# Attention kernel on one Trainium2 core: the first group's maxima computed inside the last half batch of projections

## The chip, the cores and the metric

One core of one Trainium2 chip runs the kernel. The metric is the device time of one execution in microseconds (us), the median of three runs: 2611.24 us for the kernel before (2609.54 to 2612.29).

## The reference, cut to what matters

One transformer layer with adaptive layer norm; x is 4 x 1024 x 1024 in float32.

```
mod = silu(c) @ wmod                        # six parts: sa, ca, ga, sb, cb, gb
h   = layernorm(x) * (1 + ca) + sa
q, k, v = h @ Wq, h @ Wk, h @ Wv            # 32 query heads, 8 key/value heads, head size 32
q, k = rope(q), rope(k)
att = q @ k.T / sqrt(32), causal            # 4 query heads share one key/value head
x   = x + ga * ((softmax(att) @ v) @ Wo)
h   = layernorm(x) * (1 + cb) + sb
x   = x + gb * (h @ W.T + bias + lora)
```

## The kernel before, in words

Three functions run one after the other, each with a program block of its own, and at a block's end all engines meet: `qkv` (projections), `attention`, `linear_half`.

**qkv** works on eight half batches m of 512 tokens. For each, PE multiplies twelve chunks of 128 output columns (two of k, two of v, eight of q, `project`, L502 to L514): 24 matmuls a chunk, since weights and activations are each split into a high and a low part. For the ten chunks of k and q, ACT copies the product out of PSUM (L317), DVE applies the rotary embedding (`rotate`, L402 to L411: a product, a shuffle, a product, a sum), ACT rounds to the high part (L329), POOL subtracts for the low part (L469), and SP stores both to DRAM in `qk_t` (L242). v is transposed and stored to `v_t` (L249). During half batch m the activations of m + 1 are normalized and transposed; the last half batch has nothing of that kind beside it. At the end SP waits until all stores have landed (L279 to L281).

**attention** works on 32 groups n (4 batches x 8 key/value heads, 4 query heads each). A group needs, from DRAM, stacked copies of q and k (high, high and low parts, 96 rows; `load_stack`, L643). Softmax needs each row's maximum before the exponential, so a group's scores are computed twice: first with queries on the partitions, in 38 units (`max_scores`, L968 to L984), each reduced by DVE (`take_max`, L844); the maxima are then split into high and low (L853), transposed by PE (`turn`, L1002), copied by ACT (L811) and written by SP as two more rows of the q stack (L655); then, with keys on the partitions, in 20 units (`scores`, L948) which subtract the maximum through these two rows, ACT's exponential (L792), the product with v (`values`, L986) and sums. L977 and L983 add the causal mask by a product with the identity.

The order on every engine is one list, `STEPS` (L130): first all 38 units of group 0, its turn and the 10 first units of group 1, alone; from there on each group's scores are mixed with the maxima of the next ones. `SP` first loads stacks 0 and 1, v of batch 0 and one 4 MB part of wmod (L720 to L723), then follows the list. The three PSUM banks for maxima, turns and sums are used in turn.

Of the kernel before, what the change touches and what calls it, by code (L numbers as in the profile page):

```python
# [14 lines left out]
P = 128  # L15
# [23 lines left out]
XB = 4  # L39
# [90 lines left out]
STEPS = [("max", 0, m) for m in range(NM)] + [("turn", 0)] + [("max", 1, m) for m in range(NM) if MAX_TICK[m] < 0]  # L130
STEPS += [s for n in range(NG + 1) for s in group_steps(n)]
# [29 lines left out]
def qkv(nc, consts, x_in, wq_in, wk_in, wv_in, c_in, wmod_in, silu_cols, mod_cols, rope_in, qk_out, v_out):  # L161
# [3 lines left out]
    with ExitStack() as ctx:  # L165
# [3 lines left out]
        w = [sb("w_hi", [P, NC, DC, P], F32R), sb("w_lo", [P, NC, DC, P], F32R)]  # L169
        with ExitStack() as first:  # L170
            def early(name, shape):
                return first.enter_context(nc.sbuf_tensor(name, shape, F32))

            wm = early("wm", [P, DC, 4, HALF])
            crow, erow, srow = (early(n, [B, D]) for n in ("c_rows", "c_exp", "c_silu"))
            mrows = early("mod_rows", [P, HALF])
        h = [[sb(f"h_hi{i}", [P, DC, HALF], F32R), sb(f"h_lo{i}", [P, DC, HALF], F32R)] for i in range(2)]
        qst = [sb(f"roped_hilo{i}", [P, 2, HALF], F32R) for i in range(QST)]
        vst = sb("v_rows", [P, 4, P])
        qf = [sb(f"proj_raw{i}", [P, HALF]) for i in range(QF)]  # L180
        qc, rot = sb("proj_cos", [P, HALF]), sb("proj_rot", [P, HALF])
        xt = [sb(f"x_in{i}", [P, D]) for i in range(XB)]
        rope = sb("rope", [P, 2, T])
        hf = [sb(f"h_raw{i}", [P, HALF]) for i in range(TPS)]
        stats, mv, sd = sb("stats", [P, 4, 12]), sb("mean_var", [P, 4, 2]), sb("std", [P, 4, 4])
        ident = consts[:, 0:P]
        raw = [sb(f"w_raw{i}", [P, DC, P]) for i in range(STAGES)]
# [5 lines left out]
        ups = ctx.enter_context(nc.psum_tensor("mod_turned", [P, HALF], F32))  # L193

# [15 lines left out]
        s_qs = [count(f"qk_stored{i}", 16) for i in range(QST)]  # L210
        s_vs = count("v_stored", 16)
# [10 lines left out]
        def _(sp):  # L222
# [6 lines left out]
            def load_w(c):  # L229
                i = c % STAGES  # L230
                if c >= STAGES:
                    sp.wait_ge(s_wl.sem, s_wl.at(c - STAGES + 1))
                kind, n = CHUNKS[c]
                src = {"q": wq_in, "k": wk_in, "v": wv_in}[kind]
                sp.dma_start(raw[i][:, :, :],
                             src[:, n * P:(n + 1) * P].rearrange("(k p) n -> p k n", p=P)).then_inc(s_raw[i].sem, 16)
# [15 lines left out]
            def load_wm(k):  # L252
                sp.dma_start(wm[:, k, :, :], wmod_in[k * P:(k + 1) * P, 0:4 * HALF].rearrange("p (q n) -> p q n", q=4)
                             ).then_inc(s_wm[k].sem, 16)
# [24 lines left out]
            for i in range(QST):  # L279
                sp.wait_ge(s_qs[i].sem, s_qs[i].at(len([r for r in range(NRP * HB) if r % QST == i])))  # L280
            sp.wait_ge(s_vs.sem, s_vs.at(2 * HB))  # L281

        @block.scalar
        def _(act):
# [10 lines left out]
            def w_hi(c):  # L295
                i = c % STAGES
                act.wait_ge(s_raw[i].sem, s_raw[i].at(c // STAGES + 1))
                nc.scalar.activation(w[0][:, c, :, :], raw[i][:, :, :], ACT.Copy
# [46 lines left out]
            for m in range(HB):  # L345
                for c in range(NC):
# [7 lines left out]
                    if m + 1 < HB:  # L354
# [5 lines left out]
                        for k in TURN_H.get(c, ()):  # L360
                            h_hi(m + 1, k)
                rope_hi(m, NC - 1)

        @block.vector
        def _(dve):
# [72 lines left out]
            for m in range(HB):  # L438
                for c in range(NC):
                    if m + 1 < HB:  # L440
                        for k in TURN_H.get(c, ()):
                            modulate(m + 1, k)
                    if CHUNKS[c][0] != "v":
# [9 lines left out]
        def _(pool):  # L453
            def w_lo(c):
                i = c % STAGES
                pool.wait_ge(s_wh.sem, s_wh.at(c + 1))
                nc.gpsimd.tensor_tensor(w[1][:, c, :, :], raw[i][:, :, :],
                                        w[0][:, c, :, :].bitcast(F32), ALU.subtract).then_inc(s_wl.sem, 1)
# [19 lines left out]
            for m in range(HB):  # L478
                for c in range(NC):
# [10 lines left out]
        def _(pe):  # L490
# [11 lines left out]
            def project(m, c):  # L502
# [5 lines left out]
                for k in range(DC):  # L508
                    if c == 0:
                        pe.wait_ge(s_hl.sem, s_hl.at(DC * m + k + 1))  # L510
                    for n, (a, i) in enumerate(((0, 0), (0, 1), (1, 0))):
                        last = nc.tensor.matmul(pps[e % PPS][:, :], w[a][:, c, k, :], h[m % 2][i][:, k, :],  # L512
                                                start=(k == 0 and n == 0), stop=(k == DC - 1 and n == 2))
                last.then_inc(s_pj.sem, 1)  # L514

# [14 lines left out]
            for k in range(DC):  # L530
                pe.wait_ge(s_wm[k].sem, s_wm[k].at(1))
                for q in range(4):
                    last = nc.tensor.matmul(mps[DH * q:DH * (q + 1), :], silu_cols[:, k, :], wm[:, k, q, :],
# [21 lines left out]
def attention(nc, consts, qk_in, v_in, wmod_in, silu_cols, mod_cols, modv, pre, cs, wo_in, la_in, lb_in, lw_in, s_pre, ctx_out, sums_out, inv_t):  # L555


    with ExitStack() as ctx:
# [3 lines left out]
        qs = sb("q_stack", [P, QS, G, T], F32R)  # L562
        ks = sb("k_stack", [P, QS, T], F32R)
        V = sb("v", [P, 2, TT, KV * DH])
# [4 lines left out]
        negm = sb("neg_max", [P, 2, G, TT])  # L569
        mfull = sb("neg_max_and_hi", [P, G * TT, 2])  # L570
        mhl = sb("neg_max_hilo", [P, P], F32R)
        mrow = sb("neg_max_rows", [2 * G * TT, P], F32R)
        maskS = sb("mask_q_k", [P, G, P], F32R)
        maskT = sb("mask_k_q", [P, G, P], F32R)
        identr = sb("ident_r", [P, P], F32R)
# [11 lines left out]
        def count(name, step=1):  # L587
# [3 lines left out]
        s_st = [count(f"stack_loaded{i}", 16 * 6) for i in range(QS)]  # L591
        s_v = [count(f"v_loaded{i}", 16) for i in range(2)]
        s_p1, s_mx, s_mc, s_mh, s_ml, s_mt, s_me = (count(n) for n in (
            "max_scores", "max_taken", "max_joined", "max_hi", "max_lo", "max_turned", "max_rows"))
        s_mr = [count(f"max_stacked{i}", 32) for i in range(QS)]
# [41 lines left out]
        def _(sp):  # L637
            def load_v(b):
                if b >= 2:
                    sp.wait_ge(s_pv.sem, s_pv.at(NQ * KV * (b - 1)))  # L640
                sp.dma_start(V[:, b % 2, :, :], v_in[b].rearrange("(i p) d -> p i d", p=P)).then_inc(s_v[b % 2].sem, 16)

            def load_stack(n):  # L643
                b, g, s = n // KV, n % KV, n % QS
                if n >= QS:
                    sp.wait_ge(s_p2.sem, s_p2.at(NE * (n - QS + 1)))
                for row, part in enumerate((0, 0, 1)):
                    sp.dma_start(qs[DH * row:DH * row + DH, s, :, :].bitcast(F32),
                                 qk_in[b, HEADS_Q + g, part].rearrange("(h d) t -> d h t", d=DH)).then_inc(s_st[s].sem, 16)
                for row, part in enumerate((0, 1, 0)):  # L650
                    k = DH * (g % HEADS_K)
                    sp.dma_start(ks[DH * row:DH * row + DH, s, :].bitcast(F32),
                                 qk_in[b, g // HEADS_K, part, k:k + DH, :]).then_inc(s_st[s].sem, 16)

            def stack_max(n):  # L655
                sp.wait_ge(s_me.sem, s_me.at(n + 1))
                for i in range(2):
                    sp.dma_start(qs[MHI + i:MHI + i + 1, n % QS, :, :].rearrange(
                        "a h (i n) -> a (h i) n", n=P).bitcast(F32),
                                 mrow[G * TT * i:G * TT * (i + 1), :].bitcast(F32)).then_inc(s_mr[n % QS].sem, 16)  # L660
# [841 lines left out]
```

## Time and profile before

| what | value |
|---|---|
| median of three runs | 2611.24 us |
| the profiled execution | 2611.64 us |
| its span, first to last instruction | 2609.9 us |
| PE busy | 2514.4 us (96%) |
| DVE busy | 1577.4 us (60%) |
| POOL busy | 1649.7 us (63%) |
| ACT busy | 1021.0 us (39%) |
| PE's last projection matmul ends | 614.8 us |
| first matmul of the maxima of group 0 | 635.5 us |
| first scores matmul of group 0 | 668.8 us |

PE is TensorE's matmuls and PEld its weight loads, DVE is VectorE, ACT ScalarE, POOL GpSimd, SP the engine that issues the DMAs. The granted clock of PE is given as a share of 2.4 GHz: 1.00 is 2.4 GHz and 0.50 is 1.2 GHz.

### The profile page before, as it was taken

The page shows a single profiled execution, that of the slowest core. Times are in us where ns is not written, and L with a number is a line of the kernel's source. Part 1 is how long each engine was busy: PE and PEld are TensorE (multiplying, and loading weights), DVE is VectorE, ACT ScalarE, POOL GpSimd, SP SyncE. Part 2 cuts the span into 40 slices and gives each one's busy share as a digit, 9 for nine tenths or more (in the row PEclk, how much of TensorE's full clock was granted, in tenths as well). Part 3 has the DMA queues.
Part 4 walks back from the last instruction along what each step waited for, and adds up shares of the span by engine and source line. Part 5 has one row for each costly group of instructions (what it writes and reads, how often), then busy time and mean ns, then how long its engine had stood idle before and what let it go on. Part 6 is the DMA issues. An engine that isn't in the chain of part 4 may idle for free. (4 is left out here: it accounts for less than half of the span.)

```text
span 2609.9 us, 37478 instructions
## 1 busy us (share of the span) xinstructions
PE 2514.4 (96%) x14476; PEld 1871.7 (72%) x14476; DVE 1577.4 (60%) x2509; ACT 1021.0 (39%) x1301; POOL 1649.7 (63%) x863
## 2 busy tenths in 40 slices
PE   5999999996999999999999999899899999999998
PEld 2788888885766666666666666565588788888886
DVE  4667666655766666666666666465755455454553
ACT  3333333321455665565555666465411111111110
POOL 4543333331488898988988889787555455555553
PEclk8999999997799999999999999899999999999999
DMA  7432233325324335225332335230433433333330
GB/s 277 137 114 103 99 114 113 113 89 173 95 74 131 79 81 139 76 67 144 83 91 53 71 81 161 56 79 19 161 97 97 111 91 97 108 95 105 113 89 25
DMA packets 179726, 267.53 MB, mean 103 GB/s; under 512 B 20508, under 2 KB 113884, under 8 KB 178400
## 3 DMA queue, kind: packets, MB, share of 16 engines
q1 hardware_dynamic: 179552, 265.13, 34.5%
q8 instruction: 119, 1.95, 0.3%
q14 instruction: 55, 0.45, 0.1%
HBM read 183.22 MB, written 80.81 MB: 101 GB/s over the span
## 5 line engine op out<-in xcount | busy, mean ns | idle before, releaser
L927 POOL TENSOR_TENSOR p_sum<-p_sum,p_ring 128x1024 f32<-128x1024 f32 (+2 forms) x465 | 993.9, 2171 | 188.5 <-PE ctx_ps L997 170.4
L850 DVE TENSOR_REDUCE neg_max<-scores_q 128x1 f32<-128x512 f32 (+3 forms) x1216 | 740.6, 658 | 390.8 <-PE scores_q L983 226.5
L792 ACT ACTIVATE p_ring<-scores 128x1024 f32<-128x1024 f32 (+2 forms) x512 | 463.6, 918 | 250.4 <-PE scores L965 178.9
L979 PE MATMUL scores_q<-k_stack,q_stack 96*128 96x512 f32 (+3 forms) x1536 | 467.5, 381 | 0.4 <-DVE prefetched L892 0.4
L961 PE MATMUL scores<-q_stack,k_stack 98*128 98x512 f32 (+1 forms) x1216 | 417.4, 421 | 12.7 <-ACT p_ring L792 11.8
L469 POOL TENSOR_TENSOR roped_hilo<-roped_hilo 128x512 fp32r<-128x512 f32 x80 | 104.3, 1304 | 333.2 <-ACT roped_hilo L329 333.2
L961 PEld LDWEIGHTS scores<-q_stack,k_stack 98*128 98x128 f32 x1216 | 195.5, 192 | 166.1 <-issue 96.2
L979 PEld LDWEIGHTS scores_q<-k_stack,q_stack 96*128 96x128 f32 x1536 | 284.7, 198 | 38.1 <-DVE neg_max L850 4.2
L512 PE MATMUL proj_ps<-h_hi,w_hi 128*128 128x512 f32 x768 | 304.6, 397 | 1.6 <-POOL h_lo L462 1.6
L512 PE MATMUL proj_ps<-h_hi,w_lo 128*128 128x512 f32 x768 | 300.2, 391 | 0.0
L512 PE MATMUL proj_ps<-h_lo,w_hi 128*128 128x512 f32 x768 | 300.0, 391 | 0.0
L1354 POOL TENSOR_TENSOR h_scaled<-h_scaled,mod_now 128x512 f32<-128x512 f32 x64 | 65.6, 1046 | 328.1 <-DVE h_scaled L1299 328.0
L997 PE MATMUL ctx_ps<-p_ring,v 128*32 128x512 f32 (+3 forms) x2560 | 233.0, 473 | 0.0
L1426 PE MATMUL pf<-we_hi,h_hi 128*128 128x512 f32 x512 | 201.3, 393 | 8.6 <-POOL h_lo L1358 8.6
L1426 PE MATMUL pf<-we_hi,h_lo 128*128 128x512 f32 x512 | 200.8, 392 | 0.0
L1426 PE MATMUL pf<-we_lo,h_hi 128*128 128x512 f32 x512 | 200.7, 392 | 0.0
L1379 PE MATMUL po<-wo_hi,ctx_hi 128*128 128x512 f32 x496 | 196.8, 397 | 0.0
L792 ACT ACTIVATE p_sum<-scores 128x1024 f32<-128x1024 f32 x128 | 131.1, 1025 | 164.0 <-PE scores L965 93.7
L1379 PE MATMUL po<-wo_hi,ctx_lo 128*128 128x512 f32 x496 | 194.0, 391 | 0.0
L1379 PE MATMUL po<-wo_lo,ctx_hi 128*128 128x512 f32 x496 | 193.7, 391 | 0.0
L317 ACT COPY proj_raw<-proj_ps 128x512 f32<-128x512 f32 x96 | 56.4, 587 | 333.2 <-PE proj_ps L512 333.2
L983 PE MATMUL scores_q<-mask_q_k,ident_r 128*128 128x128 f32 x768 | 175.5, 229 | 0.0
(147 smaller groups left out, 3722.3 us busy)
## 6 DMA issues: line engine op xcount, KB each, us to landing
q_stack<-qk_t SPq DMA_DIRECT2D x96, 512.0 KB, 6.9
qk_t<-roped_hilo SPq DMA_DIRECT2D x80, 512.0 KB, 2.7
x_in<-in_L_attn_resid SPq DMA_DIRECT2D x32, 512.0 KB, 6.3
prefetched<-in_L_wmod SPq DMA_DIRECT2D x4, 4096.0 KB, 13.9
ctx_t<-ctx_raw SPq DMA_DIRECT2D x64, 256.0 KB, 4.5
prefetched<-ctx_t SPq DMA_DIRECT2D x31, 512.0 KB, 4.1
prefetched<-inv_t SPq DMA_DIRECT2D x124, 128.0 KB, 5.4
k_stack<-qk_t SPq DMA_DIRECT2D x96, 128.0 KB, 8.8
```

The lines of the kernel that those rows point to most:

```text
L469: nc.gpsimd.tensor_tensor(lo, lo.bitcast(F32), qst[r % QST][:, 0, :].bitcast(F32), ALU.subtract).then_inc(s_rl.sem, 1)
L512: last = nc.tensor.matmul(pps[e % PPS][:, :], w[a][:, c, k, :], h[m % 2][i][:, k, :], start=(k == 0 and n == 0), stop=(k == DC - 1 and n = ...
L792: nc.scalar.activation(probs(n, u), src, ACT.Exp, scale=SM_SCALE).then_inc(s_ex.sem, 1)
L850: nc.vector.tensor_reduce(negm[:, lo // HALF, hs[0]:hs[-1] + 1, i:i + 1], src, AX.X, ALU.max, negate=True).then_inc(s_mx.sem, 1)
L927: nc.gpsimd.tensor_tensor(a, a, probs(n, u), ALU.add).then_inc(s_ap.sem, 1)
L961: last = nc.tensor.matmul(o[a], ks[0:KS, n % QS, j * P:(j + 1) * P], qs[0:KS, n % QS, h0:h0 + per, lo:lo + w], start=True, stop=not diag)
L979: last = nc.tensor.matmul(dst[:, a, :], qs[0:MHI, n % QS, h, i * P:(i + 1) * P], ks[0:MHI, n % QS, lo:lo + w], start=not first, stop=not d ...
L983: last = nc.tensor.matmul(dst[:, a, w - P:w], identr[:, :], maskS[:, 0, :], start=False, stop=True)
L997: last = nc.tensor.matmul(cps[DH * h:DH * (h + 1), lo - hf * HALF:HALF], V[:, b % 2, j, g * DH:(g + 1) * DH], p[:, a, :], start=(j == 0), ...
L1354: nc.gpsimd.tensor_tensor(v, v, cur[:, 4 * h:4 * h + 4, 1:2].broadcast_to([P, 4, P]), ALU.add).then_inc(s_hf.sem, 1)
L1379: last = nc.tensor.matmul(po[h][:, :], cs[slot][a][:, k, :], wo[w][:, k, h * HALF:(h + 1) * HALF], start=(k == 0 and n == 0), stop=(k == D ...
L1426: mm = nc.tensor.matmul(pf[h][:, :], hs[a][:, k, :], we[w][:, k, h * HALF:(h + 1) * HALF], start=(k == 0 and n == 0), stop=(k == DC - 1 an ...
```

## The change

The 38 maxima units of group 0, its turn, and the 10 first units of group 1 leave `STEPS` and are made in `qkv` during the last half batch (m = 7): 48 units, placed behind the matmuls of chosen k steps of chunks 1 to 11 (four a chunk, six in chunks 3 and 4). Four PSUM banks that the last half batch doesn't need hold them. DVE reduces a chunk's units ahead of that chunk's `rotate`. The turn is made at chunk 10, ACT's copy behind it, and SP writes the two rows at chunk 11.

For this the memory is laid out anew: `Early` holds tiles of `qkv` that are dead by the end of half batch 6, and `Shared` lies in the same place with stacks 0 and 1, v, the masks and the tiles of the maxima. SP fetches stack 0 in half batch 6 at chunk 9, and stack 1 and v at the start of half batch 7. The wait for all stores at the end of `qkv` goes; waits for stores are put ahead of the loads that need them, and ahead of the first exponential that writes the ring of probabilities. `attention` begins with 4 mask copies on ACT in place of 9, a memset of one k tile in place of three, and its list begins with the scores of group 0. The 4 MB part of wmod is now loaded at the start of group 1.

The diff, cut to its core:

```diff
-STEPS = [("max", 0, m) for m in range(NM)] + [("turn", 0)] + [("max", 1, m) for m in range(NM) if MAX_TICK[m] < 0]
-STEPS += [s for n in range(NG + 1) for s in group_steps(n)]
+STEPS = [s for n in range(NG + 1) for s in group_steps(n)]
+FIRST_MAXIMA = [(0, m) for m in range(NM)] + [(1, m) for m in range(NM) if MAX_TICK[m] < 0]
+UNIT_AT = {}
+for _c in range(1, NC):
+    for _k in (range(1, DC - 1) if _c in (3, 4) else range(1, DC, 2)):
+        if len(UNIT_AT) < len(FIRST_MAXIMA):
+            UNIT_AT[len(UNIT_AT)] = (_c, _k)
+TURN_FIRST = NM + 2
...
+def max_product(nc, sh, qs, ks, bank, m):
+    i, lo, w, hs, diag = MAX_UNITS[m]
+    dst = bank[:, 0:len(hs) * w].rearrange("p (h n) -> p h n", h=len(hs))
+    first = diag and w == P
+    if first:
+        nc.tensor.matmul(dst[:, :, :], sh.identr, sh.maskS[:, 0:len(hs), :], start=True, stop=False)
+    for a, h in enumerate(hs):
+        last = nc.tensor.matmul(dst[:, a, :], qs[0:MHI, h, i * P:(i + 1) * P], ks[0:MHI, lo:lo + w],
+                                start=not first, stop=not diag or first and a == len(hs) - 1)
+        if diag and not first:
+            last = nc.tensor.matmul(dst[:, a, w - P:w], sh.identr, sh.maskS[:, 0, :], start=False, stop=True)
+    last.then_inc(sh.s_p1.sem, 1)
...
 # qkv, SP
+                    if (m, c) == (HB - 2, 9):
+                        sp.wait_ge(s_tp.sem, s_tp.at(DC * HB))
+                        sp.wait_ge(s_wl.sem, s_wl.at(NC))
+                        for i in range(QST):
+                            sp.wait_ge(s_qs[i].sem, s_qs[i].at(len([r for r in range(2 * NRP) if r % QST == i])))
+                        fetch_stack(sp, sh, sh.qs[0], sh.ks[0], qk_out, 0)
+                    if (m, c) == (HB - 1, 0):
+                        sp.wait_ge(s_pj.sem, s_pj.at(NC * (HB - 1)))
+                        fetch_stack(sp, sh, sh.qs[1], sh.ks[1], qk_out, 1)
+                        sp.wait_ge(s_vs.sem, s_vs.at(4))
+                        fetch_v(sp, sh, v_out, 0)
+                    if (m, c) == (HB - 1, UNIT_AT[TURN_FIRST][0] + 1):
+                        stack_rows(sp, sh, sh.qs[0], 0)
...
-            for i in range(QST):
-                sp.wait_ge(s_qs[i].sem, s_qs[i].at(len([r for r in range(NRP * HB) if r % QST == i])))
-            sp.wait_ge(s_vs.sem, s_vs.at(2 * HB))
...
 # qkv, ACT
+                if m == HB - 1:
+                    act.wait_ge(s_hl.sem, s_hl.at(DC * HB))
+                    nc.scalar.activation(sh.identr, ident, ACT.Copy).then_inc(sh.init.sem, 1)
+                    for i in range(G):
+                        nc.scalar.activation(sh.maskS[:, i, :], consts[:, P:2 * P], ACT.Copy).then_inc(sh.init.sem, 1)
...
+                    if m == HB - 1 and c == UNIT_AT[TURN_FIRST][0]:
+                        act.wait_ge(sh.s_mt.sem, sh.s_mt.at(1))
+                        nc.scalar.activation(sh.mrow, vps[0:2 * G * TT, 0:P], ACT.Copy).then_inc(sh.s_me.sem, 1)
...
 # qkv, DVE
+                    if m == HB - 1:
+                        for i, (n, unit) in enumerate(FIRST_MAXIMA):
+                            if UNIT_AT[i][0] == c:
+                                max_reduce(nc, dve, sh, max_banks[i % len(max_banks)], n, unit)
+                                if i == NM - 1:
+                                    max_split(nc, dve, sh, 0)
                     if CHUNKS[c][0] != "v":
                         rotate(m, c)
...
 # qkv, PE: called behind the three matmuls of step (c, k) of project(7, c)
+            def first_max(i):
+                if i == 0:
+                    pe.wait_ge(sh.init.sem, sh.init.at(G + 5))
+                n, m = FIRST_MAXIMA[i]
+                if m == 0:
+                    pe.wait_ge(sh.s_st[n].sem, sh.s_st[n].at(1))
+                if i >= len(max_banks):
+                    pe.wait_ge(sh.s_mx.sem, sh.s_mx.at(i - len(max_banks) + 1))
+                max_product(nc, sh, sh.qs[n], sh.ks[n], max_banks[i % len(max_banks)], m)
+                if i == TURN_FIRST:
+                    pe.wait_ge(sh.s_ml.sem, sh.s_ml.at(1))
+                    pe.wait_ge(s_vc.sem, s_vc.at(2 * HB))
+                    nc.tensor.transpose(vps[:, 0:P], sh.mhl.bitcast(F32), ident).then_inc(sh.s_mt.sem, 1)
...
 # attention, SP
-            load_stack(0)
-            load_stack(1)
-            load_v(0)
-            load_part(0)
             for step in STEPS:
                 kind, n = step[0], step[1]
                 if kind == "scores" and step[2] == 0:
                     if n + 2 < NG:
                         load_stack(n + 2)
+                    if n == 1:
+                        load_part(0)
...
 # attention, ACT
-            nc.scalar.activation(identr[:, :], consts[:, 0:P], ACT.Copy).then_inc(init.sem, 1)
             for h in range(G):
-                nc.scalar.activation(maskS[:, h, :], consts[:, P:2 * P], ACT.Copy).then_inc(init.sem, 1)
                 nc.scalar.activation(maskT[:, h, :], consts[:, 2 * P:3 * P], ACT.Copy).then_inc(init.sem, 1)
...
+                    if n == 0 and place == 0 and not before:
+                        for i in range(QST):
+                            act.wait_ge(sh.s_qs[i].sem, sh.s_qs[i].at(len([r for r in range(NRP * HB) if r % QST == i])))
+                        act.wait_ge(sh.s_vs.sem, sh.s_vs.at(2 * HB))
...
 # attention, POOL and PE
-            nc.gpsimd.memset(ks[MHI:MHI + DH, :, :].bitcast(F32), 1.0).then_inc(init.sem, 1)
+            nc.gpsimd.memset(ks[2][MHI:MHI + DH, :].bitcast(F32), 1.0).then_inc(init.sem, 1)
...
-            pe.wait_ge(init.sem, 2 * G + 5)
+            pe.wait_ge(init.sem, G + 2)
```

## Rows read from the trace of the kernel before

**Rows 1.** Windows by stage: PE, PEld, DVE, ACT, POOL busy, granted clock, DMA share.
```profile
549.40:614.80 65.40, 65.36 (x293) 53.77 (x291) 29.80 (x50) 12.58 (x24) 12.89 (x10) 1.00 0.24 89
614.80:635.50 20.70, 0.00 (x0) 0.00 (x0) 3.32 (x8) 3.65 (x12) 5.18 (x3) 0.57 0.63 165
635.50:661.60 26.10, 24.62 (x75) 18.73 (x75) 23.39 (x42) 0.00 (x0) 0.00 (x0) 0.50 0.83 262
661.60:668.80 7.20, 7.20 (x29) 6.80 (x29) 5.12 (x9) 1.55 (x2) 0.00 (x0) 0.50 0.50 121
668.80:682.50 13.70, 13.70 (x47) 11.48 (x49) 8.01 (x13) 5.29 (x6) 0.00 (x0) 0.50 0.39 83
704.50:740.00 35.50, 35.49 (x257) 23.61 (x256) 23.69 (x43) 21.20 (x25) 31.99 (x16) 1.00 0.30 73
```

**Rows 2.** Timeline between the last projection and the first maxima: start, duration, what.
```profile
619.37 1.26 POOL L469 TENSOR_TENSOR roped_hilo<-roped_hilo 128x512 fp32r<-128x512 f32 x1 [2.11 <-ACT roped_hilo L329]
...
623.86 1.30 SPq L648 DMA_DIRECT2D q_stack<-qk_t  x3
623.86 2.65 POOL L916 MEMSET k_stack<- 32x3072 f32 x1 [3.23 <-POOLq L165]
623.88 0.31 ACT L768 ACTIVATE ident_r<-consts 128x128 fp32r<-128x128 f32 x1 [4.59 <-PEq L165]
...
625.20 1.48 SPq L652 DMA_DIRECT2D k_stack<-qk_t  x3
...
625.49 0.29 ACT L771 ACTIVATE mask_k_q<-consts 128x128 fp32r<-128x128 f32 x1
...
635.55 0.77 PE L977 MATMUL scores_q<-mask_q_k,ident_r 128*128 128x512 f32 x1 [20.79 <-DMA k_stack<-qk_t]
```

**Rows 3.** SP's wait for the landing of the stores, line L281.
```profile
L281 SPq EVENT_SEMAPHORE  x1: 2271/2271/2271, 621.1 to 621.1; - x1
```

**Rows 4.** Groups by form in 636 to 661.5 us: the most frequent of DVE's reduces.
```profile
L850 DVE TENSOR_REDUCE neg_max<-scores_q 128x1 f32<-128x512 f32 x24 | 14.8, 684 | 0.1
```

**Rows 5.** Timeline: first scores and first values of group 0.
```profile
668.80 1.16 PE L961 MATMUL scores<-q_stack,k_stack 98*128 98x512 f32 x2
...
681.94 1.31 PE L997 MATMUL ctx_ps<-p_sum,v 128*32 128x512 f32 x8
```

**Rows 6.** Timeline of PE at full clock: starts of masked maxima matmuls of 128, 256 and 512 columns.
```profile
805.07 0.45 PE L977 MATMUL scores_q<-mask_q_k,ident_r 128*128 128x512 f32 x1
...
805.98 0.33 PE L979 MATMUL scores_q<-k_stack,q_stack 96*128 96x256 f32 x1
...
808.79 0.33 PE L979 MATMUL scores_q<-k_stack,q_stack 96*128 96x256 f32 x1
...
809.02 0.33 PE L979 MATMUL scores_q<-k_stack,q_stack 96*128 96x256 f32 x1
...
1143.03 0.45 PE L979 MATMUL scores_q<-k_stack,q_stack 96*128 96x512 f32 x1
1143.31 0.22 PE L983 MATMUL scores_q<-mask_q_k,ident_r 128*128 128x128 f32 x1
1143.37 0.45 PE L979 MATMUL scores_q<-k_stack,q_stack 96*128 96x512 f32 x1
```

**Rows 7.** Waits of the queues, 600 to 640 us: who waited, total, times, longest.
```profile
SPq L242 <- POOL roped_hilo L469: 23.2, 5, 5.1
```

**Rows 8.** The page's DMA issues: count, KB each, median us to landing.
```profile
k_stack<-qk_t SPq DMA_DIRECT2D x96, 128.0 KB, 8.8
```

**Rows 9.** Windows of 1 us, columns of rows 1: where the granted clock falls and rises.
```profile
617.00:618.00 1.00, 0.00 (x0) 0.00 (x0) 0.87 (x2) 0.00 (x0) 0.26 (x1) 0.82 0.00 0
...
90.00:91.00 1.00, 0.68 (x3) 0.68 (x4) 0.00 (x0) 1.00 (x3) 0.44 (x1) 0.50 0.00 0
...
95.00:96.00 1.00, 1.00 (x5) 0.79 (x4) 1.00 (x3) 0.00 (x0) 1.00 (x1) 0.80 0.00 0
...
682.00:683.00 1.00, 1.00 (x9) 0.27 (x12) 0.69 (x1) 0.00 (x0) 0.00 (x0) 0.75 0.00 0
```

More of the change, by code:

```diff
@@ L158, in at, with __init__, sb @@
         return k * self.step
-def qkv(nc, consts, x_in, wq_in, wk_in, wv_in, c_in, wmod_in, silu_cols, mod_cols, rope_in, qk_out, v_out):
+class Early:
+    def __init__(self, nc, ctx):
+        def sb(name, shape, dt=F32):
+            return ctx.enter_context(nc.sbuf_tensor(name, shape, dt))
+        self.w_hi = sb("w_hi", [P, NC, DC, P], F32R)
+        self.xt = [sb(f"x_in{i}", [P, D]) for i in range(XB)]
+        with ExitStack() as before:
+            self.wm0 = before.enter_context(nc.sbuf_tensor("wm0", [P, DC // 2, 4, HALF], F32))
+        self.h0 = [sb("h_hi0", [P, DC, HALF], F32R), sb("h_lo0", [P, DC, HALF], F32R)]
+        self.raw = [sb(f"w_raw{i}", [P, DC, P]) for i in range(STAGES)]
+        self.hf = [sb(f"h_raw{i}", [P, HALF]) for i in range(TPS)]
@@ new lines, in fetch_stack @@
+def fetch_stack(sp, sh, qs, ks, qk_in, n):
+    b, g, s = n // KV, n % KV, n % QS
+    for row, part in enumerate((0, 0, 1)):
+        sp.dma_start(qs[DH * row:DH * row + DH, :, :].bitcast(F32),
+                     qk_in[b, HEADS_Q + g, part].rearrange("(h d) t -> d h t", d=DH)).then_inc(sh.s_st[s].sem, 16)
+    for row, part in enumerate((0, 1, 0)):
+        k = DH * (g % HEADS_K)
+        sp.dma_start(ks[DH * row:DH * row + DH, :].bitcast(F32),
+                     qk_in[b, g // HEADS_K, part, k:k + DH, :]).then_inc(sh.s_st[s].sem, 16)
@@ L779, in exp @@
                 else:
-                    _, before = ring_place(n, u)
+                    place, before = ring_place(n, u)
+                    if n == 0 and place == 0 and not before:
+                        for i in range(QST):
+                            act.wait_ge(sh.s_qs[i].sem, sh.s_qs[i].at(len([r for r in range(NRP * HB) if r % QST == i])))
+                        act.wait_ge(sh.s_vs.sem, sh.s_vs.at(2 * HB))
                     if before:
@@ L1449, in _ @@
                 sp.wait_ge(s_k, 16)
-        qkv(nc, consts, x, wq, wk, wv, c, wmod, silu_cols, mod_cols, rope, qk_t, v_t)
+        with ExitStack() as first:
+            early = Early(nc, first)
         pre = ctx.enter_context(nc.sbuf_tensor("prefetched", [P, DC + 2, D], F32))
@@ L1453, in build @@
         s_pre = [ctx.enter_context(nc.semaphore(n)) for n in ("wo_fetched", "first_ctx_fetched", "first_ctx_ready",  "lora_fetched", "lora_a_scaled")]
-        attention(nc, consts, qk_t, v_t, wmod, silu_cols, mod_cols, modv, pre, cs, wo, la, lb, lw, s_pre, ctx_t, sums_t, inv_t)
+        with ExitStack() as both:
+            sh = Shared(nc, both)
+            qkv(nc, early, sh, consts, x, wq, wk, wv, c, wmod, silu_cols, mod_cols, rope, qk_t, v_t)
+            attention(nc, sh, consts, qk_t, v_t, wmod, silu_cols, mod_cols, modv, pre, cs, wo, la, lb, lw, s_pre, ctx_t, sums_t, inv_t)
         linear_half(nc, consts, x, pre, cs, s_pre, w, bias, modv, mod_cols, ctx_t, sums_t, inv_t, out)
```

206 lines of the change are left out of this document (109 added, 97 removed).

## The prediction

> **What bounds the kernel now.** I read the table of windows by stage first. In the last half batch of projections PE is busy 65.36 of 65.40 us at a clock of 1.00, and in a steady stretch of attention 35.49 of 35.50 us [rows 1]: in both, PE is the bound. Between them it isn't. PE stands still for 20.7 us, then makes the maxima of group 0 in 26.1 us and the ten first units of group 1 in 7.2 us, all at 0.50, which is 1.2 GHz. From the last projection (614.8) to the first scores (668.8) pass 54.0 us.
>
> The timeline says what these consist of. The last chunk's way through ACT, DVE, ACT and POOL ends at 620.6 [rows 2]; SP then issues the last store and waits 2.27 us for its landing [rows 3]; the new block begins at 623.86; its copies and memsets end by 626.5, but PE is held until 635.55, and the row names the DMA of a k stack [rows 2]. Loads, not setup, end that wait. In the maxima themselves DVE is the pace: busy 23.39 of 26.1 us [rows 1], with 24 reduces of 512 columns at 684 ns and hardly any idle time [rows 4], while PE waits for banks. In 661.6 to 668.8 PE is the bound, at half clock.
>
> DVE, meanwhile, has room just before: 29.80 us busy in the 65.4 us of the last half batch [rows 1]. So the change takes work that is bound by DVE and by a DMA, alone, and puts it where PE is the bound. There it costs PE's time for it, and nothing else if DVE and SP keep up.
>
> **The change part by part.** The sum is made for the profiled execution (2611.64 us, 0.4 us above the median).
>
> 1. *Removed:* everything from 614.8 to 668.8, 54.0 us [rows 1, 2, 5].
>
> 2. *PE's time for 48 units and a transpose inside the half batch.* Prices are from start to start at full clock [rows 6]. Two masked matmul pairs of 256 columns begin 0.23 us apart (808.79, 809.02), of 512 columns 0.34 us (1143.03, 1143.37); I take 0.29 for 384 columns, between the two. A unit of four heads with 128 columns is 0.68 us: from 805.07 to 805.98 lie it and one pair of 256, so 0.91 - 0.23. A 512 without a mask costs up to the 0.28 us from 1143.03 to the mask's start at 1143.31; the 512 columns alone are 0.213 us at 2.4 GHz; I take 0.24. Group 0 has 2 units of the 128 kind, 8 pairs each of 256, 384 and 512, and 16 plain 512: 1.36 + 1.84 + 2.32 + 2.72 + 3.84 = 12.1 us. The ten of group 1 are 0.68 + 4 x 0.23 + 4 x 0.29 + 3 x 0.34 = 3.8 us. With the transpose, 16.0 us. No row shows these units between projection matmuls, so I bound it: below by the columns alone (22,528 + 6,528 over 2.4 GHz = 12.1 us), above by the 33.3 us that they take now at half clock behind DVE [rows 1]. I stay at 16.0, since rows 6 too have other matmuls before and behind.
>
> 3. *DVE beside it, costed at nothing.* DVE gets 48 reduces at 0.68 us at most, 33 us, to its 29.8: 63 us in a stage of 65.4 + 16.0 = 81.4. Per chunk of four units: PE 5.45 + 1.33 = 6.8 us, DVE 4 x 0.68 + 3.0 = 5.7. A unit waits only for the reduce four units back, which for four a chunk is the same place in the chunk before, and that reduce stands ahead of that chunk's rotate: done. Behind the reduces wait rotate, then ACT's and POOL's rounding and the store; they have three PSUM banks and three stage tiles of slack. Chunks 3 and 4, with six units, follow the v chunks, which have no rotate. If this cover were gone, each us of DVE over 6.8 a chunk would be a us of PE.
>
> 4. *SP and the loads.* Stack 0 is six DMAs, issued at chunk 9 of half batch 6: 2.8 us of SP's time by the like six from 623.86 on (1.30 + 1.48 [rows 2]), against an idle of up to 5.1 us between stores [rows 7]. Landing takes about 9 us [rows 8], and PE wants it at chunk 1 of half batch 7, about four chunks (22 us) later. Stack 1 and v (seven DMAs, some 3.3 us) go in the same way and are wanted at chunk 9. The stores of q and k behind them start at most 3 us late; rotate needs a store only three chunks later. Two rows of maxima are written at chunk 11, which ends before the block does. Cost zero; if late, PE would stand still for the lateness, not more. ACT's five mask copies (1.2 us) delay one PSUM copy by half a us, with three banks behind it. POOL's two memsets (0.9 us each, a third of the 2.65 us [rows 2]) fall into half batch 1, where POOL has most of its time free.
>
> 5. *The new boundary.* Before: PE's end to the new block 623.86 - 614.8 = 9.1 us. The landing wait of 2.3 us [rows 3] goes; the wait that replaces it stands on ACT before its third exponential, over 4 us into the block, when the store has long landed. The last unit's reduce stands ahead of the last rotate: +0.5. So 7.3 us. Then four copies on ACT: nine took 1.9 us (623.88 to 625.78 [rows 2]), 0.2 apart after a first of 0.31, so 0.9; POOL's memset takes 0.9 beside them; with 0.2 for the semaphore and the first weights, the first scores stand 1.1 us into the block. PE's gap is 8.4 us.
>
> 6. *Attention from its first scores on* is the same list. The clock will have fallen: it fell 2.8 us after PE's last matmul [rows 9]. Before, it was at 0.50 from the first scores for 13.7 us more, until 682.5 [rows 1, 9]. I take the same: its rise came 0.6 us after the first values matmuls (681.94 [rows 5]), and these stand at the same place of the list in both kernels, while the 21 us of maxima and scores before them, with PE never idle, brought no rise. The bound on the other side is under the rivals. The first table load of ACT (1.3 us) overlaps the first scores.
>
> 7. *The 4 MB part of wmod* moves from the start to group 1. It no longer shares the DMA engines with the first stacks; it will share them with stack 3, which is wanted some 26 us later, and the part itself is wanted at group 4, over 100 us later. Nothing.
>
> Sum: 54.0 - 16.0 - 7.3 - 1.1 = 29.6 us saved. 2611.6 - 29.6 = 2582.0 for an execution like the profiled one, **2581.6** against the median of 2611.24.
>
> **The rivals.**
>
> *The clock rises sooner (0.25).* After another stop, the projections begin again at 90.3 and the clock is up at about 95.4, 5.1 us later [rows 9]. Should it do so in the new ramp, 13.7 - 5.1 = 8.6 us of half-clock work shrink to no less than half: 4.3 us more, 2577.3. Against it: the same kind of work ran at 0.50 for 21 us. The Trainium skill ("TensorE: Matmul & The Clock Gate", on the clock gate) says that how busy PE has been recently sets the clock, which alone would bring it up soon after any restart; the trace agrees at 90 us and not at 661 us.
>
> *The units cost PE more between projections (0.12).* Each unit switches the array from 128 to 96 rows and to a mask, or DVE's semaphores come late now and then. At 24 to 26 us for the 48 units, about midway between 16.0 and the 33.3 of now, the gain is 20 to 22 us: 2590.
>
> *DVE becomes the bound of the last half batch, and the kernel is slower (0.03).* Place: DVE's queue, where the reduces of a chunk stand ahead of its rotate. It decides from 6.8 us of DVE a chunk on; to be slower than before, the half batch must take 111 us, 10.1 a chunk of the eleven. That needs rotate and reduces to take 1.8 times 5.7 us, as by a held-up chain over stores. At 11 us a chunk: 2611 + 10 = 2621. For it: all ten rotates wait on a chain of four engines. Against it: DVE's shuffles and reduces keep their times in every stage that I read.
>
> *The gap stays (0.02).* If the first scores had to wait again for something issued only in the new block, the 9 to 20 us of waiting would come back, and with a dearer item 2 almost all would be eaten: about 2608.
>
> **How the numbers follow.** My case has 0.58, the early clock 0.25, dearer units 0.12, slower 0.03, the gap 0.02. A measurement of this kernel can tell about 0.2%, 5.2 us, from no change. Faster by over that: 0.58 + 0.25 + 0.12 and half of the last, 0.96; within it 0.01; slower 0.03. The range takes in the early clock with a cheaper item 2 (2577.3 less 1 to 2) and reaches on the other side to item 2 at 22 us: 2575.5 to 2588. Dearer units, the gap and the slower case beyond it, and an early clock with the columns' bound, make up less than 0.2.
>
> **What would show it.** In the changed profile: the last half batch lasts 81 to 82 us with PE busy throughout at 1.00 and no idle time put down to neg_max; DVE busy some 63 us in it; no row with a wait for k_stack; PE's gap about 8.4 us; the clock at 0.50 from the gap until the first values. Wrong would be: PE waits for neg_max between projections (rival three); a first scores matmul later than 640.5; a rise of the clock 5 us after it (rival one); a stage of over 86 us with PE busy (rival two).

## The result and the profile after

The changed kernel takes 2578.49 us (median of four runs, 2577.02 to 2580.00) against 2611.76: a ratio of 0.9873, interval 0.9856 to 0.9890. Run again beside other kernels, it took 2581.36 against 2611.10: 0.9886, 0.9870 to 0.9901. So the saving is 30 to 33 us; 29.6 was forecast, at 2581.6.

Windows by stage of the changed kernel, with the columns of [rows 1]:

```profile
549.40:632.00 82.60, 82.58 (x395) 68.63 (x393) 59.00 (x103) 13.97 (x30) 14.11 (x10) 1.00 0.37 107
632.00:639.60 7.60, 0.00 (x0) 0.00 (x0) 3.71 (x7) 2.41 (x8) 3.73 (x3) 0.66 0.30 113
639.60:651.60 12.00, 11.99 (x37) 10.35 (x38) 5.94 (x9) 5.92 (x6) 0.00 (x0) 0.50 0.84 180
651.60:670.00 18.40, 18.40 (x131) 11.80 (x133) 12.90 (x25) 11.92 (x13) 14.85 (x8) 1.00 0.04 16
```

The last half batch was 65.4 us and is 82.6, with PE busy throughout at 1.00 and DVE at 59.0 us. Of the three lines between it and the first scores in [rows 1] one is left, 7.6 us.

The timeline across the boundary, to be read beside [rows 2, 5]:

```profile
631.71 0.58 ACT L442 COPY proj_raw<-proj_ps 128x512 f32<-128x512 f32 x1 [5.56 <-PE proj_ps L661]
631.75 0.22 PE L247 MATMUL turn_ps<-mask_q_k,ident_r 128*128 128x128 f32 x1
632.01 0.69 DVE L257 TENSOR_REDUCE neg_max<-turn_ps 128x1 f32<-128x512 f32 x1 [1.06 <-PE turn_ps L247]
...
636.54 1.26 POOL L612 TENSOR_TENSOR roped_hilo<-roped_hilo 128x512 fp32r<-128x512 f32 x1 [2.12 <-ACT roped_hilo L454]
...
638.61 0.95 POOL L1038 MEMSET k_stack<- 32x1024 f32 x1 [0.80 <-POOLq L280]
...
639.61 1.22 PE L1083 MATMUL scores<-q_stack,k_stack 98*128 98x512 f32 x2 [7.63 <-POOL k_stack L1038]
...
652.27 1.07 PE L1107 MATMUL ctx_ps<-p_sum,v 128*32 128x512 f32 x8
```

The first scores stand at 639.6 in place of 668.8, and the row names POOL's memset, not a DMA, as what PE waited for last. The saving to this point is 29.2 us. The span is 33.9 us shorter, so another 4.7 us came later. The account by stages stands in the table below.

Every kernel profiled, by stage (us). "Front" runs from the first projection matmul to the first scores matmul; "attention" from there to the first DMA of `linear_half`; "linear" from that to the issue of the last store but one of the output; "clock" is how long after the first scores the granted clock reached 1.00 (0: it never fell); "jump" is the longest record of the branch that closes PE's loop in `linear_half`. That branch runs three times: it jumps back twice and falls through once.

| kernel | front | attention | linear | clock | jump |
|---|---|---|---|---|---|
| before | 620.0 | 1171.6 | 745.8 | 13.7 | 7.2 |
| changed | 590.8 | 1169.9 | 743.2 | 12.0 | 6.5 |
| e1_fetch_only | 607.1 | 1170.7 | 743.8 | 12.8 | 6.7 |
| e2_end_wait | 594.0 | 1170.0 | 745.8 | 12.0 | 6.9 |
| e3_two_reduces | 606.1 | 1172.3 | 745.4 | 14.3 | 6.9 |
| e4_warm | 590.3 | 1169.0 | 739.9 | 11.0 | 0.2 |
| e5_warm31 | 591.7 | 1165.3 | 738.4 | 0 | 0.2 |
| e6_tiny26 | 590.7 | 1170.2 | 739.7 | 12.1 | 0.2 |
| e7_group1_left | 593.6 | 1169.4 | 743.1 | 11.4 | 6.2 |
| e8_part_early | 591.5 | 1168.9 | 746.4 | 11.0 | 7.3 |
| e9_tail_units | 590.8 | 1162.9 | 739.6 | 0 | 0.2 |
| e10_before_tiny26 | 621.0 | 1170.3 | 737.3 | 12.3 | 0.2 |
| e11_after_again | 591.1 | 1170.4 | 746.2 | 12.5 | 6.8 |
| e12_warm31_again | 591.7 | 1165.6 | 738.3 | 0 | 0.2 |

What is left of each span is the time up to the first projection matmul, which varied from 48.5 to 51.0 us between kernels that do the same there, and 22 to 24 us behind the issue of the last store but one.

### The profile page after: what moved, and what is told of

The parts are those of the page before. It is cut to its first block and busy times, and to the rows that moved or that the text cites. A ratio compares the mean times of both kernels' runs of the same rounds, so it can differ in the third digit from the quotient of the medians.

```text
span 2576.0 us, 37491 instructions
## 1 busy us (share of the span) xinstructions
PE 2494.8 (97%) x14476; PEld 1858.3 (72%) x14476; DVE 1581.7 (61%) x2509; ACT 1020.0 (40%) x1301; POOL 1649.5 (64%) x865
## 5 line engine op out<-in xcount | busy, mean ns | idle before, releaser
L257 DVE TENSOR_REDUCE neg_max<-scores_q 128x1 f32<-128x512 f32 (+1 forms) x1168 | 711.5, 658 | 375.6 <-PE scores_q L247 227.6
L244 PE MATMUL scores_q<-k_stack,q_stack 96*128 96x512 f32 (+1 forms) x1473 | 436.6, 371 | 0.1
L244 PEld LDWEIGHTS scores_q<-k_stack,q_stack 96*128 96x128 f32 x1473 | 265.7, 192 | 32.2 <-DVE prefetched L1014 0.9
L661 PEld LDWEIGHTS proj_ps<-h_hi,w_lo 128*128 128x128 f32 x768 | 144.7, 188 | 31.2
```

The lines of the kernel that those rows point to most:

```text
L244: last = nc.tensor.matmul(dst[:, a, :], qs[0:MHI, h, i * P:(i + 1) * P], ks[0:MHI, lo:lo + w], start=not first, stop=not diag or first and ...
L257: nc.vector.tensor_reduce(sh.negm[:, lo // HALF, hs[0]:hs[-1] + 1, i:i + 1], src, AX.X, ALU.max, negate=True).then_inc(sh.s_mx.sem, 1)
L661: last = nc.tensor.matmul(pps[e % PPS][:, :], w[a][c][:, k, :], h[m % 2][i][:, k, :], start=(k == 0 and n == 0), stop=(k == DC - 1 and n = ...
```

## The experiments

**The two halves of the change.** Only the fetch and the missing wait, with the maxima back in attention:

```diff
-STEPS = [s for n in range(NG + 1) for s in group_steps(n)]
+STEPS = [("max", 0, m) for m in range(NM)] + [("turn", 0)] + [("max", 1, m) for m in range(NM) if MAX_TICK[m] < 0]
+STEPS += [s for n in range(NG + 1) for s in group_steps(n)]
...
-                            if UNIT_AT[i] == (c, k):
-                                first_max(i)
```

> The changed kernel, but with the 48 maxima units and the turn back at the front of attention's list; the early fetch of stacks 0 and 1 and of v, the missing wait for the stores at the end of qkv and the late part of wmod stay. My account (the saving is two things: a shorter gap of PE, and work taken from a stretch bound by DVE at half clock): PE stands still for about 7.6 us after the last projection, then 26.1 + 7.2 us of maxima at 1.2 GHz as in the kernel before, so first scores near 614.8 + 7.6 + 33.3 = 655.7 us and 2594 to 2595 us, 16 us above the changed kernel and 17 below the kernel before. Rival (the DMA wait was nearly all of it): within 4 us of the changed kernel, 2579 to 2583. Rival (the fetch brings nothing by itself): 2608 or more.

Measured: 2595.33 us against 2610.45, ratio 0.9941 (0.9924 to 0.9958). Its windows:

```profile
614.80:622.50 7.70, 0.13 (x1) 0.00 (x0) 3.13 (x6) 2.63 (x7) 3.44 (x3) 0.68 0.29 109
622.50:648.60 26.10, 24.64 (x74) 18.71 (x74) 23.37 (x42) 0.02 (x1) 0.04 (x1) 0.50 0.02 9
648.60:655.90 7.30, 7.25 (x29) 6.85 (x29) 5.16 (x9) 1.55 (x2) 0.00 (x0) 0.50 0.55 123
```

The stop of 20.7 us [rows 1] is 7.7, the maxima take 26.1 and 7.3 us (26.1 and 7.2 before), although the 4 MB transfer that ran beside them is gone, and the first scores stand at 655.9. The front is 12.9 us shorter than before; moving the 48 units takes off 16.3 more.

**Each term by itself.** The stores' wait put back at the end of `qkv`:

```diff
                 store_qk(m, NC - 1)
+            for i in range(QST):
+                sp.wait_ge(s_qs[i].sem, s_qs[i].at(len([r for r in range(NRP * HB) if r % QST == i])))
+            sp.wait_ge(s_vs.sem, s_vs.at(2 * HB))
```

> The changed kernel with SP's wait for the landing of all stores put back at the end of qkv. My account: PE's gap grows from 7.6 to 9.9 us, 2580.8. Rival (the wait is hidden beside the meeting of the engines): 2578.5.

Measured: 2582.30 us (2581.56 to 2585.43), ratio 0.9891 (0.9874 to 0.9907).

```profile
644.27 1.22 PE L1086 MATMUL scores<-q_stack,k_stack 98*128 98x512 f32 x2 [10.11 <-POOL k_stack L1041]
```

PE stood still for 10.11 us, 2.5 more than the 7.63 of the changed kernel: the 2.27 us of [rows 3], visible in full. The total grew by more than was expected, 3.8 us against the changed kernel's first measurement and 0.9 against its second. The profiled execution also has a first projection 1.4 us later and a linear stage 2.6 us longer (table), neither of which the edit reaches, so the 2.5 us are read from the gap and not from the totals.

The part of wmod back at the front:

```diff
-                    if n == 1:
-                        load_part(0)
...
+            load_part(0)
             for step in STEPS:
```

> The changed kernel with the 4 MB part of wmod loaded at the front of attention's list again, ahead of stack 2, rather than at group 1. My account: stack 2 lands some 12 us later but is wanted 26 us later, so nothing changes, 2578.5. Rival (the transfer slows the ramp, or takes SP 8 us at the wrong place): 2580 or more.

Measured: 2580.17 us (2577.50 to 2582.11). Attention took 1168.9 us, no longer than in the changed kernel, so the place of this transfer costs nothing there. The median lies on the rival's side (2580 or more), but 1.7 us above the first measurement of the changed kernel and 1.2 us under its second are not told from noise; it is the stage that speaks for the account.

The ten units of group 1 left in attention:

```diff
-FIRST_MAXIMA = [(0, m) for m in range(NM)] + [(1, m) for m in range(NM) if MAX_TICK[m] < 0]
+FIRST_MAXIMA = [(0, m) for m in range(NM)]
+STEPS = [("max", 1, m) for m in range(NM) if MAX_TICK[m] < 0] + STEPS
```

> The changed kernel with only the 38 units of group 0 (and the turn) in the last half batch; the 10 first units of group 1 stand at the front of attention's list. My account: the half batch is 4.1 us shorter, the ten units take the 7.1 us at half clock that they took before, the first scores come 3 us later, 2581.5. The clock: if its rise goes by the place in the list, it comes 12 to 14 us after the first scores; rival: it goes by the time since PE began again (12 us in the changed kernel), so it comes 5 us after the first scores, and the time is 2578 to 2579.

Measured: 2582.99 us (2580.43 to 2585.63), ratio 0.9902 (0.9886 to 0.9919). The front is 2.8 us longer than in the changed kernel, where 3 had been worked out. The clock:

```profile
642.00:643.00 1.00, 1.00 (x4) 0.83 (x4) 0.92 (x3) 0.00 (x0) 0.00 (x0) 0.50 1.08 233
654.00:655.00 1.00, 1.00 (x4) 0.74 (x4) 0.64 (x1) 0.98 (x2) 0.00 (x0) 0.74 0.00 0
```

PE had begun again seven us earlier than the scores, and the rise still came 11.4 us after the first scores (643.1 to 654.5). So it does not go by the time since PE began; it goes with the place in the list, to within the 3 us over which the rises in the table spread.

**Is DVE really hidden?** Each reduce made twice:

```diff
+        self.scratch = sb("scratch", [P, G, 1])[:, :, :]
...
+        self.s_tw = count("twice")
...
+    if twice is not None:
+        if twice:
+            dve.wait_ge(sh.s_tw.sem, sh.s_tw.at(twice))
+        nc.vector.tensor_reduce(sh.scratch[:, 0:len(hs), 0:1], src, AX.X, ALU.max, negate=True).then_inc(sh.s_tw.sem, 1)
     nc.vector.tensor_reduce(sh.negm[:, lo // HALF, hs[0]:hs[-1] + 1, i:i + 1], src, AX.X, ALU.max,
                             negate=True).then_inc(sh.s_mx.sem, 1)
```

> The changed kernel with each of the 48 reduces in the last half batch made twice (the first into a tile that nobody reads). DVE then has 8 x 0.68 + 3.0 = 8.4 us of work for a chunk, against PE's 6.9. My account (DVE is hidden as long as its work for a chunk is under PE's): PE now waits for banks, the half batch takes 12 to 15 us more, 2590.5 to 2593.5. Rival (four banks and the chunks of v give slack enough): under 2582.

Measured: 2597.67 us (2596.16 to 2600.08), ratio 0.9950 (0.9934 to 0.9967), 19 us above the changed kernel and 4 above the upper end of what was expected. The total alone would speak for my account. The stages don't. Half batch 6 in the changed kernel (its last half batch and its gap stand in the section on the result):

```profile
479.50:549.40 69.90, 69.90 (x330) 58.17 (x329) 47.60 (x74) 23.26 (x38) 26.67 (x18) 1.00 0.37 111
```

and half batch 6, the last one and the gap here, the first two cut so that they hold as many matmuls:

```profile
490.90:562.40 71.50, 71.50 (x330) 58.15 (x329) 47.28 (x74) 23.29 (x38) 26.54 (x18) 1.00 0.36 109
562.40:646.20 83.80, 83.14 (x395) 68.56 (x393) 78.62 (x145) 14.02 (x30) 13.45 (x10) 1.00 0.36 106
646.20:657.10 10.90, 0.00 (x1) 0.00 (x1) 7.02 (x14) 2.45 (x8) 3.47 (x3) 0.71 0.21 80
```

The last half batch took 83.8 us against 82.6, only 1.2 more, and PE has one wait for DVE's results in it:

```profile
PE v_ps L687 <- DVE neg_max_hilo L278: 0.7, 1, 0.7
```

That is the turn; for a bank one weight load waited, 0.2 us. So PE hardly waited: the rival (slack enough) holds for the half batch, although its number, under 2582, does not. The doubling did not take DVE past PE either: DVE was busy 78.6 us of the 83.8, since reduces that stand back to back start 0.6 us apart, not 0.68. What DVE was behind came out at the boundary. Seven reduces ran between PE's end and the last rotate, from 646.4 to 650.4, and the gap is 10.9 us, 3.3 more; that had not been counted. Another 10.8 us of the front were lost ahead of the last half batch, which the doubled reduces don't reach: the same 330 matmuls of half batch 6 took 71.5 us in place of 69.9, at a clock of 1.00 and with PE busy throughout, and the half batches before it were as slow. In the thirteen other profiles it took 69.9. Of the edit, only the added tile of 16 bytes a partition, the added semaphore or the place of the code can reach these half batches; which of them does is open. So DVE is hidden at one reduce a unit, and how much more work of DVE the half batch could hide is not shown by this run.

**The clock of the ramp.** 26 matmuls in the gap, into a bank that nobody reads:

```diff
                         for k in TURN_H.get(c, ()):
                             turn_h(m + 1, k)
+            pe.wait_ge(s_pe.sem, s_pe.at(NC * HB - 2))
+            for i in range(26):
+                nc.tensor.matmul(pps[0][:, 0:512], h1[0][:, i % DC, 0:P], h1[0][:, i % DC, 0:512], start=True, stop=True)
```

> The changed kernel with 26 matmuls of 512 columns on PE behind the last projection, into a PSUM bank that nobody reads (5.9 us in the gap of 7.6 us). Theory A (the stop of PE costs its clock, and the first 12 us of scores pay for it): the granted clock stays at 1.00, the first scores stand where they did, and the ramp of group 0 is 4 to 6 us shorter, 2573 to 2574.5. Rival B (the ramp is bound by ACT's exponentials and DVE's reduces): the clock stays up and the time is 2577 to 2578.5. Rival C (the clock falls in the last 1.7 us anyway): no change.

Measured: 2573.41 us (2573.17 to 2575.62), ratio 0.9861 (0.9844 to 0.9877). The time is what theory A said, and the trace shows that theory A isn't why:

```profile
631.51 6.15 PE L722 MATMUL proj_ps<-h_hi 128*128 128x512 f32 x26
639.36 0.73 PE L1087 MATMUL scores<-q_stack,k_stack 98*128 98x512 f32 x2 [1.70 <-POOL k_stack L1042]
```

```profile
639.00:640.00 1.00, 0.64 (x4) 0.56 (x4) 0.00 (x0) 0.98 (x3) 0.30 (x1) 1.00 0.99 305
640.00:641.00 1.00, 1.00 (x6) 0.91 (x5) 0.07 (x1) 0.99 (x2) 0.00 (x0) 0.57 0.98 201
```

The extra matmuls ended at 637.7, the scores began at 639.4, and the clock fell all the same at 640.1 (a mean of 0.57 in the microsecond from 640), though PE had been at work again for 0.8 us. Attention was 0.9 us shorter than in the changed kernel, not 5. Most of the gain stands in the linear stage: 739.9 us in place of 743.2. So two things had to be told apart, and the next two kernels do it: with 31 matmuls in place of 26 (`range(31)`),

> The changed kernel with 31 matmuls of 512 columns behind the last projection instead of the 26 of e4_warm, so that PE stands still for about 0.7 us before the first scores, not 1.7. Theory A (in e4_warm the clock fell at 640.6 only because of the 1.7 us): the clock stays at 1.00 over the ramp, the stretch from the first scores to the end of attention is about 5 us shorter than in e4_warm (1164 us instead of 1168.9). Theory P (what e4_warm gained came from the jump back of the loop in linear_half, which depends on how many instructions stand before it on PE): that jump costs what it will, between 0.2 and 6.9 us, whatever the clock did. Both can hold: 2568 with a cheap jump, 2573 with a dear one. Rival (the ramp is bound by ACT and DVE): attention 1168 to 1170 with the clock up.

and with 26 of 4 columns in place of 512:

> e4_warm with its 26 matmuls cut to 4 columns each: as many instructions on PE, hardly any activity. Theory P (the place of the loop's code on PE decides the cost of its jump back): PE's jump in linear_half costs 0.2 us as in e4_warm, and the time is 2573 to 2575. Rival (the activity before attention brought the gain): the jump costs 6.5 us again, 2578.5.

Measured: e5_warm31 2569.30 us (2567.81 to 2573.54), ratio 0.9851 (0.9835 to 0.9868), and when run again as e12_warm31_again 2569.02 (2568.46 to 2570.68), ratio 0.9841 (0.9827 to 0.9854); e6_tiny26 2574.49 (2570.57 to 2576.04), ratio 0.9862 (0.9845 to 0.9878). The windows of e5_warm31:

```profile
639.00:640.00 1.00, 0.00 (x0) 0.00 (x0) 0.09 (x1) 0.73 (x4) 0.75 (x1) 1.00 1.03 387
...
647.00:648.00 1.00, 1.00 (x13) 0.62 (x15) 1.00 (x3) 0.75 (x2) 0.00 (x0) 1.00 0.99 201
```

The clock stays at 1.00, and the first values come at 647.5, 7.2 us after the first scores in place of 12.7. Attention is 1165.3 and 1165.6 us, 3.3 to 7 us under the kernels with a slow ramp (4.3 to 4.6 under the changed one). The ramp was bound by PE, and theory A is right about it once the stop is short enough: PE stood still for 1.3 us here, in e12_warm31_again and in e9_tail_units, and for 1.7 us in e4_warm, the only profile with that stop. The 31 matmuls also have a price: they end at 639.0, last of all engines before the meeting, and the front is 0.9 us longer than in the changed kernel. e6_tiny26 keeps the slow ramp (1170.2) and has the short linear stage all the same: activity has nothing to do with that part.

**The jump of the loop.** The linear part of the kernel is a loop over batches on every engine. Its branch on PE, in the kernel before, the changed one and e6_tiny26 (duration minimum/median/maximum in ns; the maximum is the first jump back, the median the second, and the minimum the time it falls through):

```profile
L1117 PEldq COMPARE_BRANCH  x3: 83/5157/7188, 2051.6 to 2422.0; - x3
```

```profile
L1227 PEldq COMPARE_BRANCH  x3: 83/4457/6488, 2020.7 to 2388.4; - x3
```

```profile
L1231 PEldq COMPARE_BRANCH  x3: 76/212/238, 2023.9 to 2386.7; - x3
```

and what PE does behind the first jump, in the kernel before, the changed one and e6_tiny26:

```profile
2058.98 1.96 PE L1416 MATMUL pt<-consts,x_normed 128*128 128x128 f32 x8 [3.23 <-issue]
```

```profile
2027.31 1.97 PE L1526 MATMUL pt<-consts,x_normed 128*128 128x128 f32 x8 [2.53 <-issue]
```

```profile
2027.91 1.03 PE L1530 MATMUL pt<-consts,x_normed 128*128 128x128 f32 x8
```

With a dear first jump PE stands still for 2.5 to 3.2 us and comes back at half clock: the two tiles beside it take 4.3 us more in the changed kernel and 6.2 more in the kernel before than the 22.7 us a tile takes otherwise, from start to start. The second jump adds 0.6 and 1.3 us. With a cheap one every tile takes 22.7. To see whether this belongs to the change at all, the same 26 small matmuls went into the kernel before, and the changed kernel ran once more beside it:

```diff
 # the kernel before, qkv, PE, at its end
+            pe.wait_ge(s_pe.sem, s_pe.at(NC * HB - 2))
+            for i in range(26):
+                nc.tensor.matmul(pps[0][:, 0:4], h[1][0][:, i % DC, 0:P], h[1][0][:, i % DC, 0:4], start=True, stop=True)
```

> The kernel before with 26 matmuls of 4 columns behind the last projection, as in e6_tiny26. Theory P: the jump of the loop in linear_half costs 0.2 us instead of 7.2, and with it the clock, so the stretch of linear_half is 5 to 6 us shorter and the time 2605, though attention is not touched. Rival (only the layout of the changed kernel can make the jump cheap): 2610 to 2611.

> The changed kernel as it is, beside the others of this call. 2578.5 again, within 1.5 us; the jump of the loop between 6.2 and 7.3 us, as in all kernels so far with this many instructions on PE.

Measured: e10_before_tiny26 2604.79 us against 2611.10, ratio 0.9977 (0.9968 to 0.9986), with a jump of 0.24 us and a linear stage of 737.3 us in place of 745.8. The kernel before, with 26 useless matmuls, is 6.3 us faster. It is a matter of what stands ahead of the loop on PE, and not of the change. e11_after_again: 2581.36 (2579.33 to 2581.78), ratio 0.9886, jump 6.8 us, linear stage 746.2; that is 1.4 us above the upper end of what was expected. All eight profiles without extra matmuls had a dear jump, from 6.2 to 7.3 us for the first and 4.5 to 5.2 for the second, and their linear stages took 743.1 to 746.4. So the 2.6 us of the profiled executions' 745.8 and 743.2 are within what one and the same kernel shows. The Trainium skill ("Runtime: NRT & Kernel Launch", on instruction fetch mechanics) says that a taken branch whose target is outside the stretch of code held at hand stalls for a fetch; that would make the cost hang on where the loop's code falls, as these runs show, but no run shows the fetch itself.

**Room left in the gap.** The four units of chunk 11 behind the last projection, their reduces behind the last rotate, and 26 matmuls behind them:

```diff
+TAIL_UNITS = range(44, 48)
...
+            for i in TAIL_UNITS:
+                first_max(i)
+            pe.wait_ge(s_pe.sem, s_pe.at(NC * HB - 2))
+            for i in range(26):
+                nc.tensor.matmul(pps[0][:, 0:512], h1[0][:, i % DC, 0:P], h1[0][:, i % DC, 0:512], start=True, stop=True)
```

> e5_warm31 with the four units of chunk 11 issued behind the last projection and reduced behind the last rotate, and 26 matmuls behind them. My account (PE has 7.6 us of room there, DVE 3 us while ACT and POOL finish the last chunk): the last projection ends 1.4 us earlier, no reduce stands ahead of the last rotate, and the first scores come 1.8 to 2.3 us earlier than in e5_warm31, 2567.3 against 2569.3. Rival (the four reduces now end last and hold up the meeting of the engines): no gain, 2569 or more.

> e5_warm31 again, beside the others of this call: 2569.3 within 1.5 us, the clock at 1.00 from the projections through the ramp, the jump 0.2 us.

Measured: 2568.16 us (2565.10 to 2569.62), ratio 0.9836 (0.9822 to 0.9849), against 2569.02 for e12_warm31_again on the same chip; the two are not told apart. The front is 0.9 us shorter than in both profiles with 31 matmuls, half of what I had worked out:

```profile
637.76 2.20 PE L728 MATMUL proj_ps<-h_hi 128*128 128x512 f32 x9
641.22 0.74 PE L1093 MATMUL scores<-q_stack,k_stack 98*128 98x512 f32 x2 [1.26 <-POOL k_stack L1048]
```

The 26 useless matmuls run until 639.96, while the last reduce ended at 638.9: now they hold up the meeting of the engines. Fewer of them might give the rest; that wasn't tried. Attention is 2.4 to 2.7 us shorter than with 31 matmuls, and nothing in the edit reaches it; its clock was at 0.50 for some 7 us near 1610 us, against some 10 in e12_warm31_again. This version and e5_warm31 beat both kernels, by 40 to 43 us against the one before.

## Why the prediction was right, step by step

The forecast of 2581.6 and its main case held: a saving of 29.6 us against 29.7 and 33.3 in two measurements, 29.2 at the first scores of the profiled execution. Part of that closeness is luck: two sizes missed in opposite ways (items 2 and 5), and the first measurement holds some 4 us from stages that the sum left alone.

1. *What bounds the stretch.* Right. e1_fetch_only shows the DMA wait as a cost of its own (12.9 us with the stores' wait), and the maxima as bound by DVE at half clock even without a transfer beside them.

2. *PE's 16.0 us for the units.* Under-sized: PE's last matmul moved from 614.8 to 632.0, 17.2 us. Priced from starts in attention, the stage's growth is 7% more; whether the units take it or the projections beside them is not told apart. The rival of dearer units (24 to 26 us) fell.

3. *DVE at nothing.* Right: DVE was busy 59.0 of the 82.6 us (63 had been worked out), and the changed kernel has no wait of PE for DVE in that half batch. The measure that went with it, that each microsecond of DVE over 6.8 a chunk would be one of PE, did not hold in e3_two_reduces: 19.6 us more of DVE's time made the half batch 1.2 us longer and the gap behind it 3.3.

4. *The loads at nothing.* Right: in the last half batch and at the boundary no row of the changed kernel has PE waiting for a stack's load.

5. *The new boundary.* 7.6 us, where 8.4 was worked out. The last unit stands behind the last projection, so the chain of the last chunk had begun before PE's last matmul ended (631.71 against 631.97), and its reduce held up the rotate by 0.3 us, not 0.5. The 1.2 us missing in item 2 and the 0.8 us too much here nearly cancel. The 2.3 us for the stores' wait are shown by e2_end_wait.

6. *The same ramp.* The size was near, 12.0 us at half clock in place of 13.7; the reason was wrong. I had put the rise down to the first values matmuls. In the changed kernel it came at 651.6, 0.7 us before them, and in e3_two_reduces about a microsecond after. Over eleven profiles it came 11.0 to 14.3 us after the first scores. What raises it at that place in the list is open; that it isn't the time since PE began is shown by e7_group1_left. The rival of an early rise fell. What the Trainium skill ("TensorE: Matmul & The Clock Gate", on the clock gate) says of recent work was too little to tell this ramp from one that rises at once.

7. *wmod at group 1 costs nothing.* Right by the stage times: attention is 1168.9 us with the part at the front and 1169.9 with it at group 1 (e8_part_early).

What the sum did not have is the linear stage. It changed by 2.6 us between the two profiled executions, and that I had taken as untouched. Nothing in the edit reaches it. Attention behind the first scores was 1.8 us shorter; by an estimate from the two stretches at 0.50 (13.7 and 12.0 us) the ramp gives 0.9 of it, and the rest has no cause shown. The first measurement was 3.7 us better than forecast and the second 0.1; the loop's stage can account for 3 of it by the profiles, but which runs of the medians had it isn't recorded.

## What to carry to other kernels

Work that waits on another engine in a stretch of its own can be nearly free inside a stretch bound by PE, as long as the other engine has room there. Sum both engines' work over the whole stretch, and look at what the other engine still has to do when PE is done: that comes out at the boundary. When a test edit makes a kernel slower, compare stage by stage between points with the same number of matmuls, the stages ahead of the edit too: of e3_two_reduces' 19 us, 10.8 lay where the doubled reduces don't reach. When a stage of the profile changes that the edit doesn't touch, look for an accident of layout there before crediting the edit, and see whether padding gives the same to the kernel before. A stop of PE that can't be removed can still be filled, so that its clock lives through it, but the filling must reach close to the next real work: a rest of 1.3 us was short enough here in three profiles, and 1.7 us was too long in one.

## What the hardware showed that I had not expected

- A loop's first jump back on PE took 0.2 us or 6.2 to 7.3 us by its record (the second 0.2 or 4.5 to 5.2), with 2.5 to 3.2 us of standing still in the two traces read and a time at half clock behind it; 26 matmuls of 4 columns ahead of it decide which. Six microseconds of 2600 hung on that.
- The clock can fall while PE works: at 640.1 in e4_warm, 2.5 us after the extra matmuls ended and 0.8 us after the scores had begun. With a stop of 1.3 us (e5_warm31, e9_tail_units) it did not.
- Scores and maxima run back to back at 1.2 GHz for 11 to 14 us (over 20 us in the kernel before, from 661.6 on) before the clock rises, where a restart at 90.3 had it back after 5.1 us [rows 9]; that one began with eight transposes, the projections following at 91.9.
- The same 330 matmuls of a half batch of projections, at 1.00 and without a pause of PE, took 69.9 us in thirteen profiles and 71.5 in e3_two_reduces, whose edit puts no instruction there. The cause is open.
